# Attention output scaled and split on POOL, group by group, in a four-layer kernel

## The chip, the cores and the metric

The kernel runs on one core of a Trainium2 chip. The metric is the device time of one execution in microseconds; the median of several runs is compared. The engines are PE (matrix products), DVE (vector), ACT (activations), POOL (general purpose) and SP, which here only issues DMAs. SBUF is the working memory of 128 partitions, PSUM the memory that PE writes, DRAM lies off chip.

## The reference, cut to what matters

Four layers of attention and feed-forward work on an x of 2 x 512 tokens and 256 features, with a context of 2 x 1024 tokens. The change lies in the first half of the first layer, an attention with 16 heads of 16 features:

```
x = x + L0_xattn(layernorm(x), ctx)
q = xn @ Wq.T + bq          k = ctx @ Wk.T + bk          v = ctx @ Wv.T + bv
weights = softmax(q k / sqrt(16))        per head
attn = weights @ v
L0_xattn = attn @ Wo.T + bo
...
x = x + L0_ffn(layernorm(x))             eight experts, all computed
```

The softmax's division is done late: the kernel takes the products of the unnormalised exponentials with v, and beside them their sums, and multiplies by the inverse of the sums afterwards.

## The kernel before

The sixteen heads of two batches are worked on as NR = 8 groups r of four heads (batch r // 4, heads 4 (r % 4) and following), each for 512 queries. The attention block (`l0_attention_phase`, L572) runs in periods. In the period of r PE computes the scores of group r (b_unit, L687, 16 units), the products with v of group r (av_unit, L700), and, in between, the scores of group r + 1 a first time in the other direction (a_tile, L731), from which DVE takes each query's maximum (L798 and L802). POOL turns the maxima into negative bf16 parts (negate, L654), PE transposes them (turn_max, L680), ACT copies the result and SP loads it into the stack of queries (load_max, L617). The last period has no a_tile. v has a column of ones beside each head, so row 16 of each head's 32 rows in the product is the sum of the exponentials. ACT copies the product into g.avs (copy_weighted, L767).

SP's queue gathers the sums of group r - 2 between load_max(r, 0) and load_max(r, 1) (gather_sums, L829, four DMAs): one row of 512 sums becomes 32 partitions of 16. The sums of group 6 are gathered in the last period, behind load_max(7, 1). When those of groups 0 to 6 are there, DVE inverts them in one instruction (L808), and SP returns them as four rows a group (return_inverses, L836). DVE then prepares constants for later layers (on_vector, L538: rounding of a weight, sums of the context), for which PE does six transposes at the block's end (L757).

A block (`nc.Block`) ends when all engines have ended their part of it. The output block follows (`l0_output_phase`, L841). For each group PE spreads the four rows of inverses over 128 partitions with a matmul against a 4 x 128 matrix of ones (spread_inverse, L875, L879), DVE multiplies (L914), ACT adds the bias of v and rounds to the high part (L871), and DVE takes the low part (L907). The projection with Wo (project, L881) is 96 matmuls of 128 x 128 with 256 columns (mm3 makes three, high and low parts, lines 73 to 75): per batch four tiles of queries, four groups, three products. DVE adds each pair of tiles to x and takes the statistics for the next norm (L923). Group 7 is gathered, inverted and returned within this block. Wo is split into its parts by POOL in the attention block, behind group 2 (split_on_pool, L928).

## Time and profile before

| | us |
|---|---|
| median of 3 runs | 1587.24 (1586.04 to 1593.71) |
| the profiled execution | 1585.52 |
| its span, first to last instruction | 1583.6 |
| PE busy in it | 1481.6 (94%) |
| DVE, ACT, POOL busy | 919.2, 704.7, 284.2 |
| mean granted clock of PE | 0.953 of 2.4 GHz |

Times of rows are microseconds from the span's start unless marked ns. A line is that of the kernel before. "busy" of PE includes matmuls that wait on their own pipeline, so the number of instructions and the granted clock are read beside it; 1.00 stands for 2.4 GHz and 0.50 for 1.2 GHz. A releaser behind an arrow is the operation that ended an idle time. Rows with "q" behind the engine (SPq, PEq) are its queue.

### The profile page before, as it was taken

Reading aid. Unit: us, or ns where it says so; the run is one execution under the profiler, and the core shown is the slowest. Engines: PE = TensorE matmul, PEld = TensorE weight load, DVE = VectorE, ACT = ScalarE, POOL = GpSimd, SP = SyncE. Lnnn points to the kernel's source line nnn. Section 1 sums busy time; section 2 is a strip of 40 time slices with the busy share of each in tenths; the row PEclk is TensorE's granted clock in tenths of the full one; section 3 lists DMA queues with packets and bytes.
Section 4 is the critical chain, followed back from the end, with each engine's and each line's share of the span. In section 5 each row is a group of like instructions: output and inputs, shape, how many; then the busy total and the mean of one; then the engine's idle time right before and its main releaser. Section 6 shows DMA issues by size and latency. Waiting matters only on the chain. (4 is left out here: it accounts for less than half of the span.)

```text
span 1583.6 us, 25401 instructions
## 1 busy us (share of the span) xinstructions
PE 1481.6 (94%) x8774; PEld 1192.1 (75%) x8774; DVE 919.2 (58%) x1691; ACT 704.7 (44%) x1101; POOL 284.2 (18%) x287
## 2 busy tenths in 40 slices
PE   5799999899999999999998799999899899998894
PEld 4444444588888988888887678888688788887883
DVE  7778887555555545555557534444566455556556
ACT  5266667244434334344342355555433343343432
POOL 2101100011222212212120123333200122120100
PEclk8899999699999999999998899999999799999997
DMA  6711210111111111111100124555111211101000
GB/s 231 230 31 32 61 31 3 33 55 47 40 60 40 41 58 40 59 40 40 60 26 14 53 75 135 144 139 139 37 54 54 74 40 40 60 26 41 1 0 27
DMA packets 49637, 95.44 MB, mean 60 GB/s; under 512 B 8559, under 2 KB 28533, under 8 KB 48693
## 3 DMA queue, kind: packets, MB, share of 16 engines
q1 hardware_dynamic: 49589, 94.79, 19.8%
q8 instruction: 32, 0.52, 0.1%
q14 instruction: 16, 0.13, 0.0%
HBM read 83.79 MB, written 10.75 MB: 60 GB/s over the span
## 5 line engine op out<-in xcount | busy, mean ns | idle before, releaser
L1238 DVE TENSOR_TENSOR hidden_l<-silu_l,up_l 128x512 f32<-128x512 f32 x176 | 121.0, 688 | 307.3 <-ACT silu_l L1178 307.3
L1178 ACT ACTIVATE silu_l<-gate_l 128x512 f32<-128x512 f32 x176 | 105.2, 598 | 426.0 <-PE up_l L75 426.0
L75 PE MATMUL out_l<-dn_hi_l,h_lo_l 128*128 128x256 f32 x704 | 199.2, 283 | 0.0
L74 PE MATMUL out_l<-dn_lo_l,h_hi_l 128*128 128x256 f32 x704 | 199.1, 283 | 0.0
L73 PE MATMUL out_l<-dn_hi_l,h_hi_l 128*128 128x256 f32 x704 | 199.0, 283 | 0.0
L798 DVE TENSOR_REDUCE maxima<-a_scores 128x1 f32<-128x512 f32 x256 | 164.4, 686 | 42.1 <-PE a_scores L736 41.3
L1210 POOL TENSOR_TENSOR gu_lo_l<-gu_raw_l,gu_hi_l 128x1024 fp32r<-128x1024 f32 x42 | 100.7, 2398 | 408.2 <-ACT gu_hi_l L1170 408.2
L1262 DVE SCALAR_TENSOR_TENSOR x_sb<-out_l,cw,x_sb 128x256 f32<-128x256 f32 x352 | 150.0, 477 | 30.6 <-PE out_l L75 25.0
L765 ACT ACTIVATE probs<-b_scores 128x1024 f32<-128x1024 f32 x128 | 131.0, 1023 | 67.0 <-PE b_scores L695 64.9
L73 PE MATMUL gate_l<-xnT_hi_n,gu_hi_l 128*128 128x512 f32 x352 | 139.9, 398 | 2.6 <-DVE xnT_lo_n L191 2.6
L1244 DVE TENSOR_TENSOR h_lo_l<-hidden_l,h_hi_l 128x512 fp32r<-128x512 f32 x176 | 139.3, 791 | 4.4
L74 PE MATMUL gate_l<-xnT_lo_n,gu_hi_l 128*128 128x512 f32 x352 | 139.4, 396 | 0.0
L75 PE MATMUL gate_l<-xnT_hi_n,gu_lo_l 128*128 128x512 f32 x352 | 138.9, 395 | 0.0
L73 PE MATMUL up_l<-xnT_hi_n,gu_hi_l 128*128 128x512 f32 x352 | 138.8, 394 | 0.0
L75 PE MATMUL up_l<-xnT_hi_n,gu_lo_l 128*128 128x512 f32 x352 | 138.6, 394 | 0.0
L74 PE MATMUL up_l<-xnT_lo_n,gu_hi_l 128*128 128x512 f32 x352 | 138.6, 394 | 0.0
L73 PEld LDWEIGHTS out_l<-dn_hi_l,h_hi_l 128*128 128x128 f32 x704 | 134.9, 192 | 1.7
L74 PEld LDWEIGHTS out_l<-dn_lo_l,h_hi_l 128*128 128x128 f32 x704 | 134.9, 192 | 1.7
L75 PEld LDWEIGHTS out_l<-dn_hi_l,h_lo_l 128*128 128x128 f32 x704 | 134.9, 192 | 0.0
L1183 ACT ACTIVATE h_hi_l<-hidden_l 128x512 fp32r<-128x512 f32 x176 | 110.2, 626 | 10.4 <-DVE hidden_l L1238 10.4
L1702 DVE TENSOR_TENSOR hidden_l<-silu_l,spread_l 128x512 f32<-128x512 f32 x64 | 44.3, 692 | 91.7 <-ACT silu_l L1629 91.7
L736 PE MATMUL a_scores<-k_stack,q_stack 96*128 96x512 bf16 x256 | 85.4, 404 | 9.6 <-DMA q_stack<-q_stacks 5.8
(369 smaller groups left out, 3030.2 us busy)
## 6 DMA issues: line engine op xcount, KB each, us to landing
gu_raw_l<-w_units SPq DMA_DIRECT2D x44, 512.0 KB, 3.7
spread_l<-cw_rows SPq DMA_DIRECT2D x64, 256.0 KB, 3.7
dn_raw_l<-w_units SPq DMA_DIRECT2D x44, 256.0 KB, 2.6
k_stack<-k_stacks SPq DMA_DIRECT2D x8, 768.0 KB, 5.7
up_raw_l<-w SPq DMA_DIRECT2D x40, 128.5 KB, 3.3
dn_raw_l<-w SPq DMA_DIRECT2D x40, 128.0 KB, 2.1
phi_a<-fside SPq DMA_DIRECT2D x8, 512.0 KB, 3.3
k_stacks<-kq_parts SPq DMA_DIRECT2D x8, 384.0 KB, 2.6
```

The costliest lines, as they stand in the source:

```text
L73: pe.matmul(out, lhs[0], rhs[0], start=start, stop=False, skip_group_check=True)
L74: pe.matmul(out, lhs[0], rhs[1], start=False, stop=False, skip_group_check=True)
L75: return pe.matmul(out, lhs[1], rhs[0], start=False, stop=stop, skip_group_check=True)
L736: pe.matmul(a_scores[:, k % 2, :], q_stack[buf][0:MAXROW, h, at:at + P], k_stack[buf][0:MAXROW, h, kh * 512:(kh + 1) * 512], start=True, s ...
L765: act.activation(probs[u % 4][:, :, :], b_scores[:, u % 2, :, :], ACT.Exp, scale=SCALE).then_inc(exp_done, 1)
L798: dve.tensor_reduce(maxima[k // 16][:, i // 2, i % 2:i % 2 + 1], a_scores[:, k % 2, :], X, ALU.max).then_inc(a_read, 1)
L1178: act.activation(silu[:, q % 2, :], gate[:, q % 2, :], ACT.Silu).then_inc(silu_done, 1)
L1183: act.activation(h_hi[s][:, fc, half * 512:(half + 1) * 512], hidden[:, q % 2, :], ACT.Copy).then_inc(h_hi_done, 1)
L1210: pool.tensor_tensor(gu_lo[s][:, :, :, :], gu_raw[s][:, :, :, :], f32(gu_hi[s][:, :, :, :]), ALU.subtract).then_inc(gu_lo_done, 1)
L1238: dve.tensor_tensor(hidden[:, q % 2, :], silu[:, q % 2, :], up[:, q % 2, :], ALU.mult).then_inc(hidden_done, 1)
L1244: dve.tensor_tensor(h_lo[s][:, fc, t], hidden[:, q % 2, :], f32(h_hi[s][:, fc, t]), ALU.subtract).then_inc(h_lo_done, 1)
L1262: last = dve.scalar_tensor_tensor(g.x[:, c, :], out[:, b, j, :], weight, g.x[:, c, :], ALU.mult, ALU.add)
```

## The change

The work of the output block for groups 0 to 6 moves into the attention block and there from PE, DVE and ACT to POOL. DVE's loop over the maxima is written out from group 3 on, and inverts the sums of one group at a time ahead of each round (`invert`). SP stores these inverses into DRAM (`store_inverse`) and loads them back, each head's row broadcast to its 32 partitions (`load_inverse`), into one of two buffers that lie in the raw weights of Wo, which are free once they are split. POOL multiplies, adds the bias, rounds to the high part and takes the low part (`normalise`), for group r - 4 behind the second maxima of group r, and for groups 4 to 6 at the block's end. DVE's constants are cut into three functions, with the inversions of groups 5 and 6 between them, and PE's six transposes move from the block's end into the last period. In the output block only group 7 is left: PE spreads its sums, not its inverses, from g.avs by a 128 x 128 matrix, DVE inverts all 512 columns, and the projection takes the group last. The high and low parts and the buffers are held during both blocks; the memory for them comes from kq_parts, which is now released after the first block.

```diff
@@ later_constants: one function for DVE becomes three
-    def on_vector(dve):
-        own = Chain(dve, dve_steps)
+    def round_rhs(dve):
...
+    def add_context(dve):
...
+    def take_turned(dve):
...
@@ l0_attention_phase
+        attn = o.attn_biased
+        wide = [o.w_raw[:, 2 * i:2 * i + 2, :].rearrange("p a e -> p (a e)") for i in range(2)]
+        inverse_stored, attn_steps, attn_done = g.sem("inverse_stored"), g.sem("attn_steps"), g.sem("attn0_split_done")
+        wide_loaded = [g.sem(f"inverse_wide_loaded{i}") for i in range(2)]
...
+                def store_inverse(r):
+                    sp.wait_ge(o.inverse_done, r + 1)
+                    sp.dma_start(g.inverses[r, :, :].rearrange("h (j i) -> (h j) i", i=S // 32), o.sums[:, r, :]).then_inc(inverse_stored, 16)
+                def load_inverse(r):
+                    sp.wait_ge(inverse_stored, 16 * (r + 1))
+                    if r >= 2:
+                        sp.wait_ge(attn_done, r - 1)
+                    else:
+                        sp.wait_ge(o.split_done, 2)
+                    for h in range(HG):
+                        sp.dma_start(wide[r % 2][32 * h:32 * h + 32, :],
+                                     g.inverses[r, h:h + 1, :].to_broadcast([32, S])).then_inc(wide_loaded[r % 2], 16)
...
                         gather_sums(sp, g, r - 2)
+                    if r >= 3:
+                        store_inverse(r - 3)
                     load_max(r, 1)
+                    if r >= 3:
+                        load_inverse(r - 3)
                     if r >= 1 and r + 2 < NR:
                         sp.wait_ge(avs_done, r + 1)
                         load_stacks(sp, g, r + 2)
                 sp.wait_ge(avs_done, NR)
                 gather_sums(sp, g, NR - 2)
-                sp.wait_ge(o.inverse_done, 1)
-                for r in range(NR - 1):
-                    return_inverses(sp, g, r)
+                for r in range(NR - 3, NR - 1):
+                    store_inverse(r)
+                    load_inverse(r)
...
+                spare = Chain(pool, attn_steps)
+                def normalise(r):
+                    pool.wait_ge(wide_loaded[r % 2], 16 * HG * (r // 2 + 1))
+                    spare.link(pool.tensor_tensor(attn[:, :], g.avs[:, r, :], wide[r % 2], ALU.mult))
+                    spare.link(pool.tensor_scalar(attn[:, :], attn[:, :], o.bv[:, r % GROUPS:r % GROUPS + 1], None, ALU.add))
+                    spare.link(pool.tensor_copy(o.attn_hi[:, r, :], attn[:, :]))
+                    pool.tensor_tensor(o.attn_lo[:, r, :], attn[:, :], f32(o.attn_hi[:, r, :]), ALU.subtract).then_inc(attn_done, 1)
+                    pool.wait_ge(attn_done, r + 1)
                 for r in range(NR):
                     negate(r, 0)
                     negate(r, 1)
                     if r == 2:
                         split_on_pool(pool, o.w_raw, o.w_hi, o.w_lo, o.loaded, o.split_done, 48)
+                    if r >= 4:
+                        for i, count in enumerate(g.all_stores):
+                            pool.wait_ge(g.parts_stored[i], count)
+                        normalise(r - 4)
+                for r in range(NR - 4, NR - 1):
+                    normalise(r)
...
                         if u == T0_AT and not last:
                             turn_max(r + 1, 0)
+                        if u == T0_AT and last:
+                            constants.on_tensor(pe)
...
-                constants.on_tensor(pe)
...
+                def invert(r):
+                    dve.wait_ge(o.sums_gathered, 16 * HG * (r + 1))
+                    dve.reciprocal(o.sums[:, r, :], o.sums[:, r, :]).then_inc(o.inverse_done, 1)
+                with dve.Fori(0, 3) as r:
                     for k in range(AU):
                         tile_max(r, k)
-                dve.wait_ge(o.sums_gathered, 16 * HG * (NR - 1))
-                dve.reciprocal(o.sums[:, 0:NR - 1, :], o.sums[:, 0:NR - 1, :]).then_inc(o.inverse_done, 1)
-                constants.on_vector(dve)
+                for r in range(3, NR):
+                    invert(r - 3)
+                    for k in range(AU):
+                        tile_max(r, k)
+                constants.start(dve)
+                invert(NR - 3)
+                constants.round_rhs(dve)
+                invert(NR - 2)
+                constants.add_context(dve)
+                constants.take_turned(dve)
@@ l0_output_phase
-        attn = sb("attn0", [P, 2, 512])
-        attn_hi, attn_lo = sb("attn0_hi", [P, NR, 512], F32R), sb("attn0_lo", [P, NR, 512], F32R)
-        inverse = ctx.enter_context(nc.psum_tensor("inverse0", [P, 4, 512], F32))
+        bv = o.bv[:, R % GROUPS:R % GROUPS + 1]
+        inverse, attn = sb("inverse_last", [P, S]), sb("attn_last", [P, S])
+        sums = ctx.enter_context(nc.psum_tensor("sums_last", [P, S], F32))
         out = ctx.enter_context(nc.psum_tensor("out0", [P, TC // 2, 2, D], F32))
-        spread_done, attn_done, added = g.sem("spread0_done"), g.sem("attn0_done"), g.sem("added_o0")
-        hi_done, lo_done, out_done = g.sem("attn0_hi_done"), g.sem("attn0_lo_done"), g.sem("out0_done")
+        spread_done, attn_done, added = g.sem("sums_spread"), g.sem("last_attn_done"), g.sem("added_o0")
+        hi_done, lo_done, out_done = g.sem("last_hi_done"), g.sem("last_lo_done"), g.sem("out0_done")
         with nc.Block() as block:
-            @block.sync
-            def _(sp):
-                gather_sums(sp, g, NR - 1)
-                sp.wait_ge(o.inverse_done, 2)
-                return_inverses(sp, g, NR - 1)
             @block.scalar
             def _(act):
-                for r in range(NR):
-                    act.wait_ge(attn_done, r + 1)
-                    act.activation(attn_hi[:, r, :], attn[:, r % 2, :], ACT.Identity, bias=bv(r)).then_inc(hi_done, 1)
+                act.wait_ge(attn_done, 1)
+                act.activation(o.attn_hi[:, R, :], attn[:, :], ACT.Identity, bias=bv).then_inc(hi_done, 1)
             @block.tensor
             def _(pe):
-                def spread_inverse(r):
-                    if r >= 4:
-                        pe.wait_ge(attn_done, r - 3)
-                    pe.matmul(inverse[:, r % 4, :], o.spread[:, :], o.inverse_rows[:, r, :], start=True, stop=True).then_inc(spread_done, 1)
-                def project(b):
+                def project(b, groups):
                     for m in range(2):
                         for j in range(2):
                             q = 2 * m + j
-                            for gr in range(GROUPS):
+                            for gr in groups:
                                 r = b * GROUPS + gr
-                                pe.wait_ge(hi_done, r + 1)
-                                pe.wait_ge(lo_done, r + 1)
-                                lhs = (attn_hi[:, r, q * P:(q + 1) * P], attn_lo[:, r, q * P:(q + 1) * P])
+                                lhs = (o.attn_hi[:, r, q * P:(q + 1) * P], o.attn_lo[:, r, q * P:(q + 1) * P])
                                 last = mm3(pe, out[:, 2 * b + m, j, :], lhs, (o.w_hi[:, gr, :], o.w_lo[:, gr, :]),
                                            j == 0 and gr == 0, gr == GROUPS - 1)
-                        last.then_inc(out_done, 1)
+                        if groups[-1] == GROUPS - 1:
+                            last.then_inc(out_done, 1)
+                pe.matmul(sums[:, :], o.spread[:, :], g.avs[:, R, :], start=True, stop=True).then_inc(spread_done, 1)
                 pe.wait_ge(o.split_done, 2)
-                pe.wait_ge(o.inverses_returned[0], 16 * (NR - 1))
-                for r in range(NR - 1):
-                    spread_inverse(r)
-                project(0)
-                pe.wait_ge(o.inverses_returned[1], 16)
-                spread_inverse(NR - 1)
-                project(1)
+                project(0, range(GROUPS))
+                project(1, range(GROUPS - 1))
+                pe.wait_ge(hi_done, 1)
+                pe.wait_ge(lo_done, 1)
+                project(1, range(GROUPS - 1, GROUPS))
             @block.vector
             def _(dve):
-                def low(r):
-                    dve.wait_ge(hi_done, r + 1)
-                    dve.scalar_tensor_tensor(attn_lo[:, r, :], attn[:, r % 2, :], bv(r), f32(attn_hi[:, r, :]), ALU.add, ALU.subtract).then_inc(lo_done, 1)
-                for r in range(NR):
-                    dve.wait_ge(spread_done, r + 1)
-                    if r >= 2:
-                        dve.wait_ge(hi_done, r - 1)
-                        dve.wait_ge(lo_done, r - 1)
-                    dve.tensor_tensor(attn[:, r % 2, :], g.avs[:, r, :], inverse[:, r % 4, :], ALU.mult).then_inc(attn_done, 1)
-                    if r >= 1:
-                        low(r - 1)
-                    if r == 2:
-                        dve.wait_ge(o.sums_gathered, 16 * HG * NR)
-                        dve.reciprocal(o.sums[:, NR - 1, :], o.sums[:, NR - 1, :]).then_inc(o.inverse_done, 1)
-                low(NR - 1)
+                dve.wait_ge(spread_done, 1)
+                dve.reciprocal(inverse[:, :], sums[:, :]).then_inc(o.inverse_done, 1)
+                dve.wait_ge(o.inverse_done, NR)
+                dve.tensor_tensor(attn[:, :], g.avs[:, R, :], inverse[:, :], ALU.mult).then_inc(attn_done, 1)
+                dve.wait_ge(hi_done, 1)
+                dve.scalar_tensor_tensor(o.attn_lo[:, R, :], attn[:, :], bv, f32(o.attn_hi[:, R, :]), ALU.add, ALU.subtract).then_inc(lo_done, 1)
...
@@ four_layers and _arrange
+        g.inverses = nc.dram_tensor("inverses", [B * GROUPS, HG, S], F32, kind="Internal").ap()
-                g.kq_parts = inner.enter_context(nc.sbuf_tensor("kq_parts", [P, 6, 3, 512], BF16))
+                    g.kq_parts = turned.enter_context(nc.sbuf_tensor("kq_parts", [P, 6, 3, 512], BF16))
+                g.out0.attn_hi = inner.enter_context(nc.sbuf_tensor("attn0_hi", [P, B * GROUPS, S], F32R))
+                g.out0.attn_biased = inner.enter_context(nc.sbuf_tensor("attn0_biased", [P, S], F32))
-            l0_output_phase(nc, g, d)
+                l0_output_phase(nc, g, d)
...
-    spread = np.zeros((HG, P), np.float32)
+    spread = np.zeros((P, P), np.float32)
     for q in range(HG):
-        spread[q, 32 * q:32 * q + 32] = 1.0
+        spread[32 * q + HD, 32 * q:32 * q + 32] = 1.0
```

## Rows read from the trace of the kernel before

**Rows 1.** By stretch: length, busy us (instructions) of PE, PEld, DVE, ACT, POOL, clock, DMA, GB/s.

```profile
279.30:291.50 12.20, 12.18 (x14) 4.43 (x14) 7.60 (x12) 4.33 (x6) 0.00 (x0) 0.50 0.02 1
291.50:296.00 4.50, 4.50 (x22) 4.47 (x22) 1.35 (x2) 0.72 (x1) 0.00 (x0) 0.50 0.01 2
296.00:299.40 3.40, 3.40 (x29) 3.33 (x28) 0.00 (x0) 0.00 (x0) 0.00 (x0) 0.97 0.02 5
334.00:340.00 6.00, 6.00 (x19) 5.03 (x19) 3.14 (x15) 1.69 (x3) 0.00 (x0) 0.50 0.37 131
```

**Rows 2.** PE in order of time: start, us, line, operation, out<-in, count, idle before.

```profile
266.25 0.61 PE L695 MATMUL b_scores<-q_stack,k_stack 99*128 99x256 bf16 x4
...
279.32 12.28 PE L879 MATMUL inverse<-inverse_rows,spread_sb 4*128 4x512 f32 x14 [3.23 <-PEq L614]
...
309.10 0.28 PE L75 MATMUL out<-wo_hi_o,attn_lo 128*128 128x256 f32 x1
```

**Rows 3.** Waits from 275.9 to 312 us: engine, tile, line, releaser: total, times, longest.

```profile
DVE attn L914 <- PE inverse L879: 12.8, 8, 7.6
```

**Rows 4.** DVE in order of time, one stretch at 133 us, others from 255.

```profile
133.09 1.29 DVE L798 TENSOR_REDUCE maxima<-a_scores 128x1 f32<-128x512 f32 x2 [0.62 <-PE a_scores L736]
...
255.96 0.17 DVE L802 TENSOR_REDUCE row_max<-maxima 128x8 f32<-128x16 f32 x1
...
265.26 0.63 DVE L542 TENSOR_REDUCE rhs_step<-rhsT_sb 128x2 f32<-128x512 f32 x1
...
268.18 2.28 DVE L556 TENSOR_REDUCE ctx_sum_sb<-ctxT_hi_sb 128x2 f32<-128x2048 f32 x1
...
278.45 0.41 DVE L565 COPY rhs_scale_sb<-a_scores 128x256 f32<-128x256 f32 x1
...
309.42 0.69 DVE L923 TENSOR_TENSOR x_sb<-x_sb,out 128x512 f32<-128x512 f32 x1 [1.37 <-PE out L75]
...
310.14 0.75 DVE L139 BATCH_NORM_STATS2 stats_sb<-x_sb 128x6 f32<-128x256 f32 x2
```

**Rows 5.** SP's issues of DMAs in order of time, last period and next block.

```profile
249.55 2.46 SPq L832 DMA_DIRECT2D sums<-avs  x4
...
260.94 2.41 SPq L832 DMA_DIRECT2D sums<-avs  x4
...
311.15 0.37 SPq L1110 DMA_DIRECT2D gu_raw_l<-w_units  x1
```

**Rows 6.** Groups by line, POOL: xcount | busy us, mean ns | idle before.

```profile
L1223 POOL TENSOR_TENSOR dn_lo_l<-dn_raw_l,dn_hi_l 128x512 fp32r<-128x512 f32 x44 | 57.1, 1298 | 179.9 <-ACT dn_hi_l L1198 179.9
...
L671 POOL COPY v_aug<-v 128x512 f32<-128x512 f32 x8 | 4.9, 609 | 0.5
```

**Rows 7.** POOL in order of time, the three rows that the text uses.

```profile
132.31 2.35 POOL L933 TENSOR_TENSOR wo_lo_o<-wo_raw_o,wo_hi_o 128x1024 fp32r<-128x1024 f32 x1
...
193.22 0.23 POOL L658 TENSOR_SCALAR neg_max<-row_max 128x8 f32<-128x8 f32 x1 [11.49 <-DVE row_max L802]
...
257.40 0.20 POOL L662 TENSOR_TENSOR neg_parts<-neg_rest,neg_parts 128x8 bf16<-128x8 f32 x1
```

**Rows 8.** DMA issues: out<-in, xcount, KB each, median us from issue to landing.

```profile
spread_l<-cw_rows SPq DMA_DIRECT2D x64, 256.0 KB, 3.7
...
sums<-avs SPq DMA_DIRECT2D x32, 2.0 KB, 1.7
...
rhsT_sb<-rhsT SPq DMA_DIRECT2D x1, 256.0 KB, 8.6
...
wr_raw_r<-wr SPq DMA_DIRECT2D x1, 64.0 KB, 1.9
```

**Rows 9.** Groups by line, DVE, 258 to 312 us.

```profile
L907 DVE SCALAR_TENSOR_TENSOR attn_lo<-attn,bv_sb,attn_hi 128x512 fp32r<-128x512 f32 x8 | 6.0, 747 | 0.1
...
L808 DVE RECIPROCAL sums<-sums 128x112 f32<-128x112 f32 x1 | 0.9, 853 | 8.4 <-DMA sums<-avs 8.4
...
L919 DVE RECIPROCAL sums<-sums 128x16 f32<-128x16 f32 x1 | 0.2, 244 | 0.0
```

More of the change, by code:

```diff
@@ L567, in later_constants, with start @@
     c = Shared()
-    c.on_sync, c.on_tensor, c.on_vector = on_sync, on_tensor, on_vector
+    def start(dve):
+        nonlocal own
+        own = Chain(dve, dve_steps)
+    own = None
+    c.on_sync, c.on_tensor, c.start = on_sync, on_tensor, start
+    c.round_rhs, c.add_context, c.take_turned = round_rhs, add_context, take_turned
     return c
@@ L802, in tile_max @@
                         dve.tensor_reduce(row_max[k // 16][:, :], maxima[k // 16][:, :, :], X, ALU.max).then_inc(row_max_done, 1)
-                with dve.Fori(0, NR) as r:
+                def invert(r):
+                    dve.wait_ge(o.sums_gathered, 16 * HG * (r + 1))
+                    dve.reciprocal(o.sums[:, r, :], o.sums[:, r, :]).then_inc(o.inverse_done, 1)
+                with dve.Fori(0, 3) as r:
                     for k in range(AU):
                         tile_max(r, k)
-                dve.wait_ge(o.sums_gathered, 16 * HG * (NR - 1))
-                dve.reciprocal(o.sums[:, 0:NR - 1, :], o.sums[:, 0:NR - 1, :]).then_inc(o.inverse_done, 1)
-                constants.on_vector(dve)
+                for r in range(3, NR):
[8 more added lines that the diff above has]
+                constants.take_turned(dve)
 def l0_output_buffers(nc, ctx, g):
@@ L819, in l0_output_buffers @@
     o.w_raw, o.w_hi, o.w_lo = split_weights(nc, g, ctx, "o0", "wo0", [P, GROUPS, D])
-    o.spread = sb("spread_sb", [HG, P])
+    o.spread = sb("spread_sb", [P, P])
     o.bv = sb("bv0_sb", [P, GROUPS])
     o.sums = sb("sums0", [P, NR, S // 32])
-    o.inverse_rows = sb("inverse_rows", [HG, NR, S])
+    o.attn_lo = sb("attn0_lo", [P, NR, S], F32R)
     o.loaded, o.split_done = g.sem("o0_loaded"), g.sem("o0_split_done")
     o.sums_gathered, o.inverse_done = g.sem("sums_gathered"), g.sem("inverse0_done")
-    o.inverses_returned = [g.sem(f"inverses_returned{i}") for i in range(2)]
 def gather_sums(sp, g, r):
@@ L833, in gather_sums @@
                      g.avs[32 * h + HD:32 * h + HD + 1, r, :]).then_inc(g.out0.sums_gathered, 16)
-def return_inverses(sp, g, r):
-    last = r == B * GROUPS - 1
-    sp.dma_start(g.out0.inverse_rows[:, r, :], g.out0.sums[:, r, :]).then_inc(g.out0.inverses_returned[last], 16)
 def l0_output_phase(nc, g, d):
     NR = B * GROUPS
+    R = NR - 1
     o = g.out0
```

3 lines of the change are left out of this document (1 added, 2 removed).

## The prediction

> **What bounds the kernel now.** The page's slices show PE busy nearly everywhere, so I looked for a place where PE is busy with little to show for it, and then read only the stretch that the change touches: the end of the attention block and the output block (275 to 311 us). First the busy time by stretch [rows 1]: from 279.3 to 291.5 us PE is busy 12.18 of 12.20 us, but with 14 instructions, and its granted clock is 0.50, the lower level (1.2 GHz). These are the seven spreads of the inverse sums (L879), two instructions each, 12.28 us in PE's order of time [rows 2], so 1.75 us a group. Then the waits [rows 3]: DVE's products (L914) wait 12.8 us for those spreads and for nothing else. So this block is bound by PE, by spreads first and by the 96 projection matmuls behind them: 22 start in 4.5 us at 0.50, then 29 in 3.4 us at 0.97 [rows 1], a pitch of 0.205 and 0.117 us. PE starts the block at 279.32 [rows 2], 0.46 us after DVE's last constant ended at 278.45 + 0.41 = 278.86 [rows 4]; SP's first load of the next block is issued at 311.15 [rows 5]. The stage to be shortened is these 31.8 us. A block ends for all engines together, so the last engine sets each edge: DVE the first, and DVE's last statistics (310.14 + 0.75 = 310.89, [rows 4]) the second, 0.26 us before the next block.
>
> **The end of the attention block.** Here POOL becomes the engine to watch. One group's normalise is four dependent POOL operations on 128x512: two with two tensors, 1.30 each; one cast, 0.61 as the copy of that size [rows 6]; one addition of a column, for which there is no row at this size: between 0.61 (one tensor read) and 1.30 (two), taken as 0.65 since it reads one. With four gaps of 0.07 that is 4.1 us, at most 4.8. Groups 0 to 2 run in periods 4 to 6, where POOL idles 11.5 us between a half's five small operations and the next half's [rows 7]; 7 us stay free before the next maximum is turned, so nothing queued behind (negate, and through it PE's turn_max) is late. The other four groups fall into the last period, which starts for POOL at 257.60 [rows 7].
>
> SP's order decides them. load_max(7,1) ended at 260.94, where the gather of group 6 stands now [rows 5]; ahead of that gather comes load_inverse(4). Four issues take 2.46 us there [rows 5], 0.6 each. A 64 KB load lands 1.9 after issue, a gathered row 1.7 [rows 8]. The 8 KB store into DRAM has no row with a landing: 1.7 at least, 3.7 (the 256 KB broadcast) at most, taken as 2.0, near the smallest transfer. So: load 4 issued by 263.4, landed 264.7; gather 6 issued by 265.85, landed 266.95; inverted on DVE (0.24, [rows 9]) by 267.2; store 5 landed 267.85; load 5 issued by 270.25, landed 271.55; store 6 landed 272.25; load 6 issued by 274.65, landed 275.95. POOL: group 3 ends at 261.8, group 4 at 268.85, group 5 at 275.7, group 6 at 280.1. DVE ends earlier: its last wait, for the sums of group 6, ends at 267.2, then the context sums and the rest, 268.18 to 278.86 = 10.7 us [rows 4], give 277.9. So POOL ends the block, and PE starts at 280.1 + 0.46 = 280.55: **1.25 us later** than now. With all DMA terms and the addition at their upper ends group 6 ends at 285.95 (+7.1); if POOL is early DVE sets 277.9 (-0.5).
>
> PE's six transposes of the constants move into the last period, behind unit 9, which starts at 266.25 [rows 2]. They wait for DVE's rounding, which can now start when the maxima end (255.96 + 0.17) and needs 0.24 + 2.92 us (265.26 to 268.18) [rows 4]: ready at 259.3, or 263.4 if it is held for a whole normalise. 3 us are left, so this costs nothing; without that cover PE would wait and the last period would grow by the difference.
>
> **In the loop before.** Each period's head gets a reciprocal on DVE, 0.24 us [rows 9], five times, and the branch back goes away. Behind it stand the maxima, and PE behind them. As upper end all of it and a semaphore shows, 1.5 us; as lower end the branch, which no row prices, gives back twice that, -1.2 us. DVE has short pauses between pairs of maxima (0.62 us at 133, [rows 4]) that absorb part of it: I take **0.4 us**. SP gets five more issues a period, 3 us, in front of load_max(r,1) (one) and of load_stacks (four); between the end of one gather, 252.0, and the next one at 260.94 SP issues a single load [rows 5], so they are hidden. DVE's maxima read PSUM while POOL works: two of them took 1.29 us beside a 2.35 us POOL subtraction at 132 us [rows 4, 7], which is 0.65 each in step. I add nothing.
>
> **The output block.** Removed: seven spreads on PE (12.28), the wait on returned inverses and seven groups of DVE and ACT work. New order from 280.55: one spread of the last group's sums, two instructions, 1.75 as now, ends 282.3. Then 96 matmuls. At the old pitch, 22 in 4.65 us at 1.2 GHz and 74 at 0.1175 = 8.7 us: last one starts near 295.55, its result is there 0.32 later as now (309.10 to 309.42, [rows 2, 4]). The last group's chain runs beside: reciprocal of 512 columns, from 853 ns at 112 and 244 at 16 [rows 9] 6.3 ns a column, 3.4 us (PSUM source not shown; at least 0.75 as other 128x512 steps); product, ACT and DVE 0.75 each at most [rows 9]: done by 288.3, while PE needs it after 84 matmuls, at 294.2. Six us of cover. After PE, DVE has two additions with statistics left, since the last group's 12 matmuls finish both halves within 0.7 us: 2 x 1.47. Block end 295.14 + 2.94 + 0.26 = **298.35** instead of 311.15: 12.8 us less, the 1.25 included.
>
> The clock is the open term here. What the rows show is that the level stayed at 0.50 through 12.2 us of spreads and rose 4.5 us into the projection [rows 1]. The Trainium skill, TensorE: Matmul & The Clock Gate, What's actually happening, says that the throttled level is the default and that activity releases it. By that rule the spreads, PE busy throughout, should have released it; the trace doesn't bear this out. By the rule the rise would be counted from the new spread, 8 matmuls would go faster, and the block would end 0.7 us earlier. I take the row's 4.5 us from the first projection matmul, and keep 0.8 us as the lower end.
>
> **Sum.** 12.8 - 0.4 = 12.4 us. Of the profiled execution (span 1583.6 and 1.9 around it, 1585.52) 1573.1 us is left; it lies 1.7 under the median of the runs, 1587.24, from which the forecast is **1574.8 us**.
>
> **Rivals.** (1) POOL's tail takes the place of what was removed: each of the two round trips behind gather 6 (store, load) at the upper ends, POOL ends 285.95, 5.85 later than taken: 1580.6. For it: four normalises in one 23 us period, and each load waits for its store to land. Against: small transfers land in 1.7 to 1.9 us here [rows 8]. The Trainium skill, GPSIMD Engine Reference, Engine selection, advises against two-input elementwise work on GpSimd as about twice as slow; the rows give 1298 against 747 ns for such a step [rows 6, 9], and by them it decides only in this period. (2) The clock stays at 1.2 GHz for all 96 matmuls: 74 x 0.0875 = 6.5 us more, 1581.3. For it: a new gap of 4 us before the block; against: it rose after a gap of 3.2 us [rows 2]. (3) The gain is partly given back in the experts' layer: at 334 to 340 us the clock is at 0.50 under full load [rows 1]; such a stretch costs half its length, 3 us: 1577.8, or if this one vanishes 1571.8. (4) Slower: DVE's new wait at the head of a period. The gathered sums of group 5 land at 249.55 + 1.9 + 1.7 = 253.1 and DVE comes at 256.1 [rows 4, 5], 3 us to spare. If a gather lands later than 4.7 us after issue, the maxima, and PE behind them, stall five times; above 7.2 us each the 12.4 us are gone. At the 8.6 us that the 256 KB load of rhsT took [rows 8], 3.9 x 5 = 19.5 us: 1594.3. Against it: all 32 gathers are summed up by 1.7 us, and the added loads go out 12 us before them.
>
> **How the numbers follow.** Forecast 0.68, rival 1 0.14, rival 2 0.06, rival 3 0.08, rival 4 0.04. A measurement of this kernel can tell about 0.5% (7.9 us) from no change, so the bounds are 1579.3 and 1595.2. Faster: the forecast, most of rival 3 and, as its time is an upper end, more than half of rival 1: 0.84. Within: 0.13, the rest of these, rival 2 and a small rival 4. Slower: 0.03. The range takes in rival 1 and the clock either way (-0.8, -3): 1570 to 1581.
>
> **What would show it.** Right: in the changed profile the output block is some 17.8 us, with one pair of spread instructions and no PE wait for the last group's parts; POOL's last subtraction ends within 1 us of the block's end at 280; DVE's maxima keep 0.65 us in step and the last period begins for POOL within 1.5 us of 257.6; PE doesn't wait at the transposes. Wrong: PE's first matmul of the output block after 283 (rival 1), a granted clock of 0.50 beyond 5 us of projection (rival 2), DVE waiting for sums in the loop (rival 4), or a last period that begins after 259.5.

## The result: 1.0% faster, and the profile after

The changed kernel takes 1571.9 us (median) against 1587.6 for the kernel before on the same chip, a ratio of 0.9898 with a 95% interval of 0.9878 to 0.9917, so 13 to 19 us less; a first comparison gave 1571.4 against 1586.6, the same ratio. The forecast was 1574.8 us, 12.4 us less. The profiled execution took 1573.16 us, its span is 1571.2.

The stage that the prediction singled out, from TensorE's first instruction of the output block to SyncE's first load of the next one, was 31.8 us [rows 2, 5] and is 297.50 - 281.14 = 16.4 us. By stretch (columns as in [rows 1]):

```profile
276.10:281.10 5.00, 0.06 (x4) 0.00 (x0) 2.19 (x5) 0.60 (x1) 4.28 (x4) 0.97 0.00 0
281.10:284.20 3.10, 3.06 (x8) 2.06 (x9) 0.97 (x1) 0.00 (x0) 0.00 (x0) 0.50 0.00 0
284.20:288.00 3.80, 3.80 (x34) 3.80 (x33) 3.08 (x2) 0.66 (x1) 0.00 (x0) 1.00 0.00 0
288.00:294.80 6.80, 6.80 (x60) 6.80 (x58) 3.86 (x8) 0.07 (x1) 0.00 (x0) 1.00 0.01 2
```

The 14 instructions at 0.50 of [rows 1] are gone; 3 us at 0.50 are left. A second stretch at 0.50 is gone with them, which neither [rows 1] nor the prediction has. In the kernel before, TensorE waited 0.92 us in all for the parts of group 7, and behind that wait the clock was low again:

```profile
303.00:306.30 3.30, 3.30 (x15) 3.30 (x16) 2.54 (x6) 0.00 (x0) 0.00 (x0) 0.50 0.00 0
```

In the first row of the changed kernel PE does nothing for 5 us while POOL is busy for 4.28: POOL has become the engine that sets the block's first edge. TensorE in order of time, against [rows 2], from the six transposes in the last period to the last projection matmul:

```profile
267.53 0.44 PE L533 MATMUL a_scores<-ident_sb,rhsT_sb 128*128 128x128 f32 x2
...
268.24 0.60 PE L747 MATMUL b_scores<-q_stack,k_stack 99*128 99x256 bf16 x4
...
281.14 2.05 PE L936 MATMUL sums_last<-avs,spread_sb 128*128 128x512 f32 x2 [4.99 <-PEq L629]
282.20 1.20 PE L73 MATMUL out<-wo_hi_o,attn_hi 128*128 128x256 f32 x1
283.20 0.42 PE L74 MATMUL out<-wo_lo_o,attn_hi 128*128 128x256 f32 x1
...
294.77 0.28 PE L75 MATMUL out<-wo_hi_o,attn_lo 128*128 128x256 f32 x1
```

POOL in order of time (start, length, line, operation, idle time before it), its last period:

```profile
257.85 1.38 POOL L705 TENSOR_TENSOR attn_biased<-avs,wo_raw_o 128x512 f32<-128x512 f32 x1
...
264.63 1.27 POOL L705 TENSOR_TENSOR attn_biased<-avs,wo_raw_o 128x512 f32<-128x512 f32 x1 [1.65 <-DMA wo_raw_o<-inverses]
...
270.62 1.27 POOL L705 TENSOR_TENSOR attn_biased<-avs,wo_raw_o 128x512 f32<-128x512 f32 x1 [1.02 <-DMA wo_raw_o<-inverses]
...
275.68 1.27 POOL L705 TENSOR_TENSOR attn_biased<-avs,wo_raw_o 128x512 f32<-128x512 f32 x1
...
279.37 1.26 POOL L708 TENSOR_TENSOR attn_lo<-attn_biased,attn_hi 128x512 fp32r<-128x512 f32 x1
```

Groups 4 and 5 wait for their loads, group 6 doesn't: the last row ends at 280.63, 0.51 us before PE starts. By line, POOL, 100 to 285 us (mean ns behind the bar):

```profile
L706 POOL TENSOR_SCALAR attn_biased<-attn_biased,bv_sb 128x512 f32<-128x512 f32 x7 | 11.0, 1574 | 0.7
L705 POOL TENSOR_TENSOR attn_biased<-avs,wo_raw_o 128x512 f32<-128x512 f32 x7 | 9.0, 1286 | 3.2 <-DMA wo_raw_o<-inverses 2.7
...
L707 POOL CAST attn_hi<-attn_biased 128x512 fp32r<-128x512 f32 x7 | 4.3, 611 | 0.5
```

VectorE against [rows 4]: the inverse of group 5 behind the last maxima, the rounding of the experts' constants beside POOL's group 3, the only wait (5.58 us, for group 6's sums), its last constant, which ends at 278.40, 2.2 us ahead of POOL, and the block's reciprocal and last statistics:

```profile
256.13 0.24 DVE L860 RECIPROCAL sums<-sums 128x16 f32<-128x16 f32 x1
...
258.13 1.38 DVE L547 TENSOR_SCALAR rhsT_sb<-rhsT_sb 128x512 f32<-128x512 f32 x1
...
266.61 0.25 DVE L860 RECIPROCAL sums<-sums 128x16 f32<-128x16 f32 x1 [5.58 <-DMA sums<-avs]
...
277.99 0.41 DVE L569 COPY rhs_scale_sb<-a_scores 128x256 f32<-128x256 f32 x1
283.23 3.36 DVE L947 RECIPROCAL inverse_last<-sums_last 128x512 f32<-128x512 f32 x1 [4.83 <-PE sums_last L936]
...
296.49 0.75 DVE L139 BATCH_NORM_STATS2 stats_sb<-x_sb 128x6 f32<-128x256 f32 x2
```

SyncE's issues against [rows 5]: load 4, gather 6, load 5, load 6, next block.

```profile
261.20 1.74 SPq L650 DMA_DIRECT2D wo_raw_o<-inverses  x4
262.98 2.45 SPq L896 DMA_DIRECT2D sums<-avs  x4
...
267.17 1.70 SPq L650 DMA_DIRECT2D wo_raw_o<-inverses  x4
...
270.67 2.51 SPq L650 DMA_DIRECT2D wo_raw_o<-inverses  x4
297.50 0.35 SPq L1141 DMA_DIRECT2D gu_raw_l<-w_units  x1
```

### The profile page after: what moved, and what is told of

Its sections match the earlier page's. It is cut to its first block and busy times, and to the rows that moved or that the text cites. A ratio compares the mean times of both kernels' runs of the same rounds, so it can differ in the third digit from the quotient of the medians.

```text
span 1571.2 us, 25226 instructions
## 1 busy us (share of the span) xinstructions
PE 1468.6 (93%) x8760; PEld 1186.7 (76%) x8760; DVE 916.3 (58%) x1683; ACT 700.1 (45%) x1094; POOL 317.8 (20%) x315
```

## The experiments

A few us are hard to tell by total time: over all these profiles, what follows the next block's first load took 1269.6 to 1278.5 us, with the same instructions. Two lengths from each trace are steadier, and the verdicts rest on them: the **attention**, from the first to the last of ScalarE's eight copies of weighted values, and the **tail**, from the last copy to SyncE's first load of the next block.

| kernel | median us | ratio to before (95%) | attention us | tail us |
|---|---|---|---|---|
| before, two profiles | 1587.6 | 1 | 167.62, 167.62 | 35.80, 35.67 |
| changed, two profiles | 1571.9 | 0.9898 (0.9878 to 0.9917) | 167.14, 167.17 | 21.28, 21.26 |
| e_unroll | 1583.3 | 0.9978 (0.9964 to 0.9992) | 166.35 | 33.98 |
| e_dve | 1575.6 | 0.9917 (0.9897 to 0.9937) | 167.17 | 23.30 |
| e_spreads | 1585.9 | 0.9991 (0.9971 to 1.0010) | 167.19 | 35.87 |
| e_pooltail | 1578.6 | 0.9930 (0.9912 to 0.9947) | 167.17 | 27.39 |
| e_gather1 | 1571.6 | 0.9885 (0.9864 to 0.9907) | 167.17 | 22.83 |
| e_gather2 | 1592.1 | 1.0010 (0.9992 to 1.0028) | 185.91 | 22.22 |
| e_warm | 1572.3 | 0.9895 (0.9876 to 0.9915) | 167.18 | 19.98 |
| e_best | 1567.2 | 0.9867 (0.9845 to 0.9889) | 167.16 | 16.66 |
| e_best2 | 1565.9 | 0.9865 (0.9844 to 0.9887) | 167.00 | 16.40 |

The kernel before stood at 1587.6 to 1589.2 us beside these kernels; the ratios are to the runs beside each. By the traces the change took 14.47 us off the tail and 0.47 off the attention, 14.9 together, within the 13 to 19 of the times.

### r_after and r_before: both kernels again

> The changed kernel again, unedited, for its ratio and for a second profile. Both theories: 1571 to 1572 us against 1585 to 1587 before, a ratio of 0.990. What the second profile is for: in the first one the attention begins 1.35 us later than in the kernel before (first copy of a group's sums at 109.1 us against 107.7) and the layers behind the output block take 1.75 us longer (576.0 against 574.2 us from the next block's first load to the second load of the last layer). If both are a matter of the clock granted in that execution, they move or vanish in this one; if they belong to the change, they stand again within 0.3 us.

> The kernel before again, unedited, for a second profile. From the last copy of weighted values to the next block's first load 35.8 us as in the first profile, the periods 25.29 us. The first copy of weighted values stands at 107.7 us in the first profile and at 107.6 where only VectorE's loop is written out, but between 107.9 and 110.4 in eight profiles with the change: if this one gives 107.5 to 107.8 again, the change has a cost of some 1 us ahead of the attention that no step of the argument has; if it gives over 108, it is the clock of an execution.

Tail and attention repeat within 0.13 us. The first copy of weighted values came at 108.3 us in the second profile of the changed kernel and at 107.55 in the second of the kernel before. Without the change three profiles give 107.55 to 107.73; with it ten give 107.6 to 110.4, mean 108.6. The clock differs there: from 53 to 60 us it was 0.70 and 0.72 in the profiles before and 0.58 and 0.63 in those after. So the expectation's test points to some 1 us lost ahead of the attention, but e_best2, which has the whole change, stands at 107.61. This stays open. The 1.75 us in the layers behind don't stand as a cost of the change: what follows the next block's first load took 1272.4 us in both profiles before and 1273.7 in both after, but 1271.7 to 1272.1 in e_best, e_best2, e_warm and e_gather1. These two stretches are also why the profiled executions differ by 12.4 and 12.8 us only, where the medians differ by 15.2 and 15.7.

### e_spreads: the spreads put back, the work left on POOL

```
+                for r in range(NR - 1):
+                    pe.matmul(spare[:, :], o.spread[0:HG, :], g.avs[0:HG, r, :], start=True, stop=True)
                 project(0, range(GROUPS))
```

> The changed kernel with seven more TensorE products of four rows (128x512, the shape that the kernel before used to spread its inverses) ahead of the first projection matmul; their result isn't used, and all of the multiplication and splitting stays where the change put it. Theory (what the change took off the path is the time of these products at the lower clock, 12.3 us for 14 passes in the kernel before): from the last copy of weighted values to the next block's first load 21.3 us become 32 to 36, and the time grows by 11 to 14 us, to 1583 to 1586 us. Rival (the path of the block ran through VectorE's and ScalarE's work of the groups, and TensorE's products would fit beside it): less than 5 us of growth.

TensorE in order of time:

```profile
282.50 2.04 PE L937 MATMUL sums_last<-avs,spread_sb 128*128 128x512 f32 x2 [4.95 <-PEq L629]
284.48 12.31 PE L940 MATMUL sums_spare<-avs,spread_sb 4*128 4x512 f32 x14
296.72 0.58 PE L73 MATMUL out<-wo_hi_o,attn_hi 128*128 128x256 f32 x1
...
302.64 0.35 PE L73 MATMUL out<-wo_hi_o,attn_hi 128*128 128x256 f32 x1
```

The tail grows by 14.6 us to that of the kernel before, the median by 14.0 (on another chip): 12.3 for the products and the rest for the clock, whose lower level lasts until the matmul at 302.64, the 28th; in the changed kernel it lasted for five. The rival falls: nothing hides these products. That the tail comes out equal to that of the kernel before is in part chance, as the low clock falls elsewhere: there it covered 20 matmuls and then the 15 or 16 behind the wait for group 7, here 27 in one stretch.

### e_dve: the spreads gone, the work back on VectorE and ScalarE

The inverses are loaded, broadcast, into the place of the high parts, and the output block multiplies and splits all eight groups:

```
-                        normalise(r - 4)
...
+                for r in range(NR):
...
+                    scale = inverse[:, :] if r == R else f32(o.attn_hi[:, r, :])
+                    dve.tensor_tensor(attn[:, r % 2, :], g.avs[:, r, :], scale, ALU.mult).then_inc(attn_done, 1)
...
```

> The changed kernel with the work of groups 0 to 6 taken back from POOL: the inverses are still stored and loaded back broadcast in the loop (into the place of the high parts), so that no TensorE spread is left but that of the last sums; the multiplication, high and low parts of all eight groups run on VectorE and ScalarE in the output block, as before. Theory A (what the change gains is the spreads that it takes off TensorE; VectorE's work had been hidden behind them): the block starts about 2 us earlier than in the changed kernel, as POOL's tail is gone (VectorE's constants end it at about 278.4 us), VectorE needs 8 x 1.45 + 3.4 = 15 us from there, the last 12 matmuls follow: last matmul at 295 to 297 us (changed kernel 294.8), 1571 to 1575 us, so that 11 to 15 of the 15 us stay. Theory B (the gain is that POOL takes the work out of the block): most of it goes, 1579 to 1586 us.

VectorE in order of time, its first products and its last low part:

```profile
277.79 1.29 DVE L954 TENSOR_TENSOR attn_last<-avs,attn_hi 128x512 f32<-128x512 f32 x2 [0.30 <-PEq L629]
...
293.08 0.75 DVE L941 SCALAR_TENSOR_TENSOR attn_lo<-attn_last,bv_sb,attn_hi 128x512 fp32r<-128x512 f32 x1 [0.79 <-ACT attn_hi L913]
```

The tail is 23.30 us, 2.0 more than in the changed kernel and 12.4 less than before. VectorE's chain takes 16.0 us (15 expected), but the block starts 1.50 us after the last copy instead of 4.92, as no POOL tail is in its way. Theory A stands: by far the most of the gain comes with the spreads off TensorE; that POOL does the work is worth 2 us.

### e_pooltail: five more operations behind POOL's last group

```
+                column, again = o.bv[:, 0:1], g.avs[:, NR - 2, :]
+                spare.link(pool.tensor_scalar(attn[:, :], again, column, None, ALU.add))
+                spare.link(pool.tensor_scalar(attn[:, :], again, 1.5, None, ALU.add))
+                spare.link(pool.tensor_scalar(attn[:, 0:256], again[:, 0:256], column, None, ALU.add))
+                spare.link(pool.tensor_tensor(attn[:, :], again, column.to_broadcast([P, S]), ALU.add))
+                spare.link(pool.tensor_copy(attn[:, :], again))
```

> The changed kernel with five more operations on POOL behind its last group, chained, their results unused: an addition of a column per partition to 128x512 numbers, the same with a number in place of the column, the same column on 128x256, an addition of two 128x512 operands of which one is the column repeated, and a copy of 128x512. Prices as the disputed step has them: 1.57 us is what the column on 128x512 took in the changed kernel (0.65 in the prediction); if that is two operands' speed (1.27) plus something for the column, the number in its place takes 0.6 to 0.8 and the repeated column 1.27; if it is the operation, both scalar forms take 1.57, and 0.8 to 0.9 on half the width. Sum with gaps 5 to 6.3 us. Theory (POOL's tail alone sets the block's start): the time grows one for one, by 5 to 7 us, to 1576.5 to 1579. Rival (another engine or the front of the block has slack): by less than 3 us.

POOL in order of time, the five operations:

```profile
279.85 1.56 POOL L730 TENSOR_SCALAR attn_biased<-avs,bv_sb 128x512 f32<-128x512 f32 x1
281.50 1.49 POOL L731 TENSOR_SCALAR attn_biased<-avs 128x512 f32<-128x512 f32 x1
283.08 0.92 POOL L732 TENSOR_SCALAR attn_biased<-avs,bv_sb 128x256 f32<-128x256 f32 x1
284.09 1.04 POOL L733 TENSOR_TENSOR attn_biased<-avs,bv_sb 128x512 f32<-128x512 f32 x1
285.19 0.61 POOL L734 COPY attn_biased<-avs 128x512 f32<-128x512 f32 x1
```

The tail grows by 6.1 us, one for one with POOL's six. The price is the scalar operation's own: 1.49 us with a number, 1.56 with a column, 0.92 on half the width, while the column as a second operand repeated along the row takes 1.04, less than the scalar form and less than two full operands (1.27).

### e_best: POOL's last group given to VectorE

Two of the four context sums also move into VectorE's idle 5.6 us:

```
+                constants.context_sums(dve, 0)
                 invert(NR - 2)
...
+                own.link(dve.tensor_tensor(scaled, g.avs[:, R, :], scaled, ALU.mult))
+                own.link(dve.tensor_scalar(o.attn_hi[:, R, :], scaled, o.bv[:, R % GROUPS:R % GROUPS + 1], None, ALU.add))
+                own.link(dve.scalar_tensor_tensor(o.attn_lo[:, R, :], scaled, o.bv[:, R % GROUPS:R % GROUPS + 1], f32(o.attn_hi[:, R, :]), ALU.add, ALU.subtract))
```

> The changed kernel with two edits at the end of the attention: two of the four sums over the context run on VectorE ahead of the inverse of group 6, where it sat idle for 5.6 us, and group 6 is multiplied and split by VectorE behind its constants (three instructions, 0.7 + 0.4 + 0.75 us) instead of by POOL (5.0 us). Theory (POOL's tail alone sets the start of the output block, 280.6 us, ahead of VectorE at 278.4): POOL ends at about 275.6, VectorE at 276.5 to 278, the block starts 2.5 to 4 us earlier, and the time falls by as much: 1567.5 to 1569 us. Rival (the block is bound by its own work or by TensorE's clock, so that an earlier start is given back): within 1 us of the changed kernel, 1570.5 to 1572.

TensorE in order of time:

```profile
278.26 1.10 PE L947 MATMUL sums_last<-avs,spread_sb 128*128 128x512 f32 x2 [1.83 <-PEq L632]
278.80 0.68 PE L73 MATMUL out<-wo_hi_o,attn_hi 128*128 128x256 f32 x1
279.31 0.29 PE L74 MATMUL out<-wo_lo_o,attn_hi 128*128 128x256 f32 x1
```

POOL ends at 275.86, VectorE at 277.72. The tail is 4.6 us shorter than in the changed kernel, the median 4.7; the theory had 2.5 to 4. The block starts 1.76 us after the last copy instead of 4.92: 3.2 of the 4.6. The rest is the clock: behind an idle time of 1.83 us instead of 4.99 the sums take 1.10 us instead of 2.05, and no matmul runs at the lower level.

### e_warm: TensorE kept busy ahead of the block

```
                 av_unit(NR - 1, (NR - 1) % 3, BU - 1)
+                pe.wait_ge(o.split_done, 2)
+                for _ in range(4):
+                    pe.matmul(b_scores[:, 0, 0:2, :].rearrange("p h q -> p (h q)"), o.spread[:, :], g.avs[:, 0, :], start=True, stop=True, skip_group_check=True)
```

> The changed kernel with four products of 128x512 (two passes of 0.53 us each at the upper level) on TensorE behind its last weighted values, where it sits idle for 5.0 us; their result isn't used, and the block's start isn't moved. In the changed kernel the first product of the block (last sums) takes 2.05 us after that idle time and the first five projection matmuls run at the lower level; where the idle time was 1.6 to 1.8 us, the same product took 1.10 us and the matmuls behind it ran at the upper one. Theory (the idle time ahead of the block costs TensorE its clock there): the block starts at the same place, the last sums take 1.1 us, and from the last copy to the next block's first load it takes 1.2 to 1.6 us less than 21.3, about 1570 us. Rival (the clock fell for another reason, such as the time since the last busy stretch): the sums still take 2.0 us and nothing changes.

TensorE in order of time:

```profile
275.28 3.70 PE L813 MATMUL b_scores<-avs,spread_sb 128*128 128x512 f32 x8
280.51 1.10 PE L939 MATMUL sums_last<-avs,spread_sb 128*128 128x512 f32 x2 [1.52 <-PEq L629]
```

The block starts 5.09 us after the last copy, as late as in the changed kernel, but at 1.00, and the tail is 1.3 us shorter. So the clock's part of e_best is shown in the trace; the medians can't show it (0.9895 and 0.9898).

### e_unroll: VectorE's loop written out in the kernel before

```
-                with dve.Fori(0, NR) as r:
+                with dve.Fori(0, 3) as r:
                     for k in range(AU):
                         tile_max(r, k)
+                for r in range(3, NR):
+                    for k in range(AU):
+                        tile_max(r, k)
```

> The kernel before with one edit: VectorE's loop over the groups' maxima runs for three groups and is written out for the other five, as in the changed kernel; no inverse is moved. Theory (the loop's turn itself costs VectorE about 0.26 us a group, on the path of the attention): groups 4 to 8 take 25.03 us each instead of 25.29, in all 1.0 to 1.5 us less, 1584 to 1586 us against 1585 to 1587. Rival (the shorter periods of the changed kernel come from something else, such as where the queues or POOL now stand): periods stay at 25.2 to 25.3 us and the time is that of the kernel before within 0.3 us.

VectorE at the head of a period, in the kernel before:

```profile
205.37 0.17 DVE L802 TENSOR_REDUCE row_max<-maxima 128x8 f32<-128x16 f32 x1
205.78 2.57 DVE L798 TENSOR_REDUCE maxima<-a_scores 128x1 f32<-128x512 f32 x4 [0.24 <-PE a_scores L736]
```

and in e_unroll:

```profile
204.41 0.17 DVE L802 TENSOR_REDUCE row_max<-maxima 128x8 f32<-128x16 f32 x1
204.64 1.29 DVE L798 TENSOR_REDUCE maxima<-a_scores 128x1 f32<-128x512 f32 x2
```

From row_max's start to the next maxima's is 0.41 us with the loop's turn and 0.23 without, and behind the turn two tiles more stand ready (four maxima in a row). The attention is 1.27 us shorter; the medians (1.3 to 5.7 us less than before) agree with this but are too wide to show it. The trace puts the idle time down to TensorE's tiles, but it goes with the turn. The 1.8 us in this profile's tail are the clock: it fell one spread later and rose earlier (0.93 from 292 to 296 us, 0.50 and 0.53 in the two profiles before).

### e_gather1 and e_gather2: the sums 2.5 and 4.9 us later

The diff is that of e_gather1; e_gather2 has range(2), and 2 in place of the factor 1 in the wait.

```
+                        for i in range(1):
+                            for h in range(HG):
+                                sp.dma_start(late_sums[32 * h:32 * h + 32, r - 2, i, :],
+                                             g.avs[32 * h + HD:32 * h + HD + 1, r - 2, :]).then_inc(o.sums_gathered, 16)
                         gather_sums(sp, g, r - 2)
...
-                    dve.wait_ge(o.sums_gathered, 16 * HG * (r + 1))
+                    dve.wait_ge(o.sums_gathered, 16 * HG * (r + 1 + 1 * min(r + 1, NR - 2)))
```

> The changed kernel with each group's gather of its sums (four transfers, 2.45 us of SyncE's queue) issued twice, the first time into a spare place; VectorE's inverse waits for both. In the changed kernel the gather is issued about 177.1 us and lands near 178.8, and VectorE reaches the inverse at 181.0, so that it has 2.2 us to spare. Theory (VectorE waits for an inverse's sums only when these are later than its own last maxima): 2.45 us later is at the edge, 0 to 0.4 us a group, in all 0 to 2 us. Rival (the queue has room, or the gather's delay holds up the maxima's rows or the stacks behind it): no change at all in the periods, or over 1 us a group.

> As the kernel with each gather twice, but three times, so that the sums land 4.9 us later than in the changed kernel and 2.5 to 2.8 us behind VectorE's arrival at the inverse. Theory: each of the five inverses in the loop stalls VectorE that long, and as the maxima and TensorE's tiles behind it pace the attention, each period grows from 25.03 us by about 2.5, in all 10 to 14 us, 1582 to 1586 us. Rival (TensorE has two tiles ahead and other units to run, so that the stall is caught up in the same period): less than 4 us in all.

With one more gather no inverse waits and the attention is 167.17 us, as in the changed kernel (the tail's 1.6 us more are 20 matmuls at the lower level instead of five). With two more, VectorE in order of time:

```profile
192.84 0.25 DVE L865 RECIPROCAL sums<-sums 128x16 f32<-128x16 f32 x1 [2.25 <-DMA sums<-avs]
...
197.38 1.29 DVE L856 TENSOR_REDUCE maxima<-a_scores 128x1 f32<-128x512 f32 x2 [1.91 <-PE a_scores L795]
```

and TensorE:

```profile
193.69 0.39 PE L795 MATMUL a_scores<-k_stack,q_stack 96*128 96x512 bf16 x1 [1.86 <-DVE maxima L856]
...
194.54 1.06 PE L752 MATMUL b_scores<-q_stack,k_stack 99*128 99x256 bf16 x4
```

Six inverses wait 2.2 to 2.6 us each; the five in the loop make 11.5, and the attention grows by 18.7. The periods are 28.6, 29.9, 30.2, 28.1 and 27.3 us instead of 25.0 to 25.2. In the last of these the growth is the stall alone; in the others TensorE's clock falls behind it (the four products at 194.54 take 1.06 us, elsewhere 0.60; 0.90 granted from 136.7 to 196.8 us, 1.00 from 224.9 on), which costs 1 to 3 us more. The theory's mechanism holds, its size was low by that. The profile is of the slowest run: the ten took 1585.0 to 1596.3 us, so that the clock's part needn't be the same in each.

### e_best2: two more edits

e_best with VectorE's loop written out for all groups, and on POOL

```
-                    spare.link(pool.tensor_scalar(attn[:, :], attn[:, :], o.bv[:, r % GROUPS:r % GROUPS + 1], None, ALU.add))
+                    spare.link(pool.tensor_tensor(attn[:, :], attn[:, :], o.bv[:, r % GROUPS:r % GROUPS + 1].to_broadcast([P, S]), ALU.add))
```

> The kernel with the two edits at the end of the attention (group 6 on VectorE, two context sums ahead of its inverse), with two more: VectorE's loop is written out for all eight groups, and POOL adds the column as a second operand repeated along the row (1.04 us measured) in place of the scalar form (1.56). Theory: POOL's tail no longer sets the block's start, so that the 0.5 us a group stay off the path; the first period of the attention goes from 25.18 to 25.03 us as the later ones; in all 0.2 to 0.8 us less than that kernel, 1566 to 1567 us, and from the last copy to the next block's first load 16.7 us as there. Rival (POOL's shorter use of the memory that it shares with VectorE makes the rounding of the experts' constants shorter and moves the block): 16.0 us or less.

The first period is 25.04 us instead of 25.18, the tail 16.40. With 1565.9 us and 0.9865 it is the fastest kernel here, 6.0 us under the changed one by the medians, which are of two chips, and 5.0 by attention and tail; from e_best the measurement can't tell it.

## Why the prediction was right, step by step

**What bounds.** Right, and tested: with the spreads put back the tail is that of the kernel before. Without them, but with the work on VectorE, 12.4 of 14.5 us stay. The size is partly luck: the traces have 14.9 us less where 12.4 were forecast. Up to the seventh copy of weighted values the changed kernel gained 1.2 us where 0.4 were to be lost. Behind that copy it gained 13.8 where 12.8 were forecast: a short stretch of low clock gave 1.4 us more, and a later start of the block took 0.4 of them.

**The end of the attention block.** That POOL's tail sets the edge is right (e_pooltail, e_best), and so is its place: the end was put 22.5 us after the head of POOL's last period (257.6 to 280.1) and came after 22.8 (257.85 to 280.63). But two terms behind it were mis-sized and cancelled. The column's addition takes 1.57 us, not 0.65, and lies outside the bounds of 0.61 to 1.30: they held the operation for something between one and two operands read, and it is neither. The Trainium skill, GPSIMD Engine Reference, Engine selection, has one-input work on GpSimd as "roughly line-rate"; a copy (0.61, half of two operands' 1.27) fits that, the scalar form (1.49 to 1.61) doesn't. Against it the round trips were shorter: the four transfers of loads 4 and 5 are issued in 1.7 us, not 2.46 (those of load 6 took 2.51), and a store lands 1.7 us after its issue, not 2.0, so that POOL had no wait for load 6, which the sum took for the last to arrive. Measured from the seventh copy (258.36 us before, 258.53 after), TensorE started 1.65 us later than before (22.61 instead of 20.96); 1.25 was forecast.

The transposes were put at nothing, as their data would be there; it was (TensorE reached them at 267.53 us without a wait). They still take TensorE's time, 0.71 us until 268.24, and the last period has none to spare: from the seventh to the last copy the changed kernel takes 17.69 us and the kernel before 16.99. By the trace nothing of this reaches the total: the last copy ends at 276.82 us and POOL, which sets the edge, at 280.63. The 0.7 us only move from the tail to the attention in the table.

**In the loop.** The step that failed in sign: +0.4 was taken, and the five periods got 1.18 us shorter (126.47 to 125.29), at the lower bound of -1.2. The loop's turn, which no row priced, costs about 0.26 us a period (e_unroll: 1.27 us), and the reciprocals cost nothing visible (the same five periods of e_unroll, which has none, take 125.21 us). That the table's attention is only 0.5 us shorter is the transposes' 0.7.

**The output block.** Forecast 17.8 us, measured 16.4. The difference is the clock: five projection matmuls ran at the lower level, not 22. This is a draw: in e_gather1, whose block is the same, there were 20, and the stage took 17.75 us. The last group's sums were sized about right: forecast 1.75 us at the lower level, and in e_spreads the next product starts 1.97 us behind them. Reciprocal (3.36 us, 3.4 forecast) and the chain behind it are covered by some 4.6 us. The prediction's pitch of 0.205 us at the lower level came from counting starts in a window; in order of time it is 0.213 (e_gather1), so that rival 2 would have been 7.1 us dearer, not 6.5. By the Trainium skill, TensorE: Matmul & The Clock Gate, What's actually happening, activity releases the clock. The trace doesn't bear that out for these products: 12.3 us of four-row products with TensorE busy throughout were granted 0.50 again in e_spreads, and the prediction did well to go by the row.

**The rivals.** POOL's tail by slow round trips: no, DMAs were faster than taken. The clock at 1.2 GHz for all 96 matmuls: in no profile. A stretch given back in the experts' layer: what follows the block varies by 9 us over the profiles of like kernels, so no such cost can be shown or excluded. The wait of an inverse: it didn't come, and its threshold stands near 2.5 us of delay (no wait at 2.45 us, 2.2 to 2.6 us of wait at 4.9), where the rows gave 3; beyond it, it is dearer than priced: 18.7 us in the profile of e_gather2, where five stalls of 2.3 us would be 11.5 by the prediction's count, as the clock adds to them.

## What to carry to other kernels

Ask what an instruction costs in its stage: seven small products were 12.3 us of a 31.8 us block, and taking them off the bounding engine was worth more than where the rest of the work went. When work moves to a slower engine beside a loop, its last group becomes the new edge; give that one to an engine that is idle there (4.7 us here) and mind how long TensorE stands idle ahead of the block. For a step that is to be hidden ask not only when its data are ready, but also whether its own engine has a slot: the six transposes put TensorE's last copy 0.7 us later, and this stayed free because POOL set the block's edge.

## What the runs showed of the hardware

- POOL's tensor_scalar on 128x512 takes 1.49 to 1.61 us, 2.5 times a copy (0.61) and more than two full operands (1.27); the column repeated as a second operand takes 1.04.
- VectorE's scalar operation on 128x512 in place takes 0.43 us alone and 1.38 beside POOL's group 3, and an addition on 128x1 takes 1.15 instead of 0.16, while its maxima, read from PSUM, stay at 1.29 for two. The Trainium skill, SBUF — State Buffer, Who interferes with whom, gives the rule: the two engines share a pair of ports, which a scalar operation of VectorE can take and an addition of two operands in SBUF takes for reading, while a reduction on this chip never contends. The trace agrees: the addition of 1.15 us ends at 276.96, just behind POOL's product (275.68 to 276.95).
- The granted clock at the block's first product was 0.50 behind idle times of 3.2 us (both profiles before) and 4.95 to 11 us, and 1.00 behind 1.5 to 1.8 us (e_dve, e_best, e_best2, e_warm). In e_unroll, behind 3.25 us, the first spread ran at 0.96 and the clock fell to 0.50 with TensorE busy at the next. In the loop of e_gather2, behind idle times near 2 us, it fell in some periods and not in others.
- A turn of VectorE's loop costs about 0.26 us, which the trace shows as a wait for TensorE.
